# Linear blocks on one core: v's projection in two pieces around the attention's product, and chunk 1's high products ahead of the low ones

## The chip, the cores and the metric

The kernel runs on one core of a Trainium2 chip. The metric is the device time of one execution in microseconds (us). Before the change three timed runs took 3326.6, 3329.98 and 3334.91 us, so the median is 3329.98 us.

## The reference

The program computes four layers on 16 sequences of 512 tokens of width 128. The change touches only the third, a stack of eight blocks of linear attention with a feed-forward part:

```python
for i in range(8):                       # NUM_BLOCKS; D = 128, FF = 512
    residual = x
    Q = fmap(x @ Wq[i] + bq[i])          # fmap(t) = elu(t) + 1
    K = fmap(x @ Wk[i] + bk[i])
    value = x @ Wv[i] + bv[i]
    KV = einsum('nsh,nsh->nh', K, value)
    Ksum = sum(K, axis=1)
    Z = 1.0 / (Q * Ksum[:, None, :] + 1e-6)
    V = Q * KV[:, None, :] * Z
    attn_out = gelu(V @ Wo[i] + bo[i])
    x = _ln(attn_out + residual, ln1_s[i], ln1_b[i])
    residual = x
    h = gelu(x @ W1[i] + b1[i])
    ff_out = gelu(h @ W2[i] + b2[i])
    x = _ln(ff_out + residual, ln2_s[i], ln2_b[i])
```

## The kernel before

`linear_blocks` (from line 2471) holds each sequence of the state as a tile of 128 features x 512 tokens in `XC`. There are 8 blocks x 16 sequences = 128 steps g, and one program for each engine, written as `part(g, old, on)`. They run as a software pipeline of six stages: in step g the engines project q, k and v of item g, do the attention's output and first norm of item g - 1, the second half of that norm and the feed-forward part of item g - 2, its last chunk and y2 of g - 3, the second norm of g - 4, and the last scaling and the write of the state of g - 5. `on(k)` says that item g - k exists. The order of the calls in `part` is the order of the engine's instructions; nothing reorders them. Semaphores order the engines against each other.

On TensorE (PE), a step is, before the change: k's and q's projection (each three fp32r products of 512 columns: high x high, high x low, low x high part; `project`, L2620 to L2622), z1's turn (`turn_z1`, four transposes into M1, L2654), v's projection, the last chunk of the feed-forward output of g - 3 (`down`, L2703), the attention's product wo (`attention_out`, one f32 product, recorded as two, L2662), chunk 0's two high products (`up_high`, L2688, L2689), z2's turn (`turn_z2`, L2675), chunk 0's low product (`up_low`, L2694), the same for chunk 1, y2's turn (L2647) and y1's turn (L2668), chunks 2 and 3, and three chunks of `down`.

What the other engines do in a step, as far as it is spoken of below:
- ScalarE (ACT): lt and rt (a logarithm and an exponential), the exponentials ek and eq (L2788, L2793), a table load (L2796), ao, the gelu of wo's product in M1 (L2802), the write of the state from M2 (XC, L2808), then the gelus of h and ff.
- VectorE (DVE): z1 (L2939), att (L2956), x1 out of z1's turn in M1 (L2964), z2 (L2939), ek's minimum (L2974), eq's minimum (L2976), fk (L2978), eq + 1 (L2981), kv with V (L2984), the statistics of y1 in M1 (L2931, L2934), fq (L2992), the statistics of y2 in M2.
- GpSimd (POOL): the high part of a state (L2860), the high and the low half of x1 (L2870, L2873), y1 = ao + state (L2886), the low part of the state (L2863), the powers for the norms (L2850, L2852), y2 (L2897).

Three tiles in PSUM are used by turns. M1 holds z1's turn, wo's product and y1's turn; `attention_out` waits for `x1_ready` before it writes M1. M2 holds z2's and y2's turn; `turn_y2` waits for `x_ready`, the write of the state. H has two halves, for even and odd chunks. V is waited for by kv on VectorE and, through `v_filled`, by POOL one step later and by SyncE once in a block: it loads the next block's `wqkv` (L3060) when all 16 projections of v are done.

Of the kernel before, what the change touches and what calls it, by code (L numbers as in the profile page):

```python
# [37 lines left out]
def ds(start, size):  # L38
    return bass.ds(start, size)
# [2431 lines left out]
def linear_blocks(nc, C, R, XC, NBLK, NB):  # L2471
# [8 lines left out]
    with ExitStack() as ctx:  # L2480
        def sb(name, shape, dt=F32):
            return ctx.enter_context(nc.sbuf_tensor("lb_" + name, shape, dt))

        def ps(name, shape, dt=F32):
            return ctx.enter_context(nc.psum_tensor("lb_" + name, shape, dt))

        def sem(name):
            return C["sems"].enter_context(nc.semaphore("lb_" + name))

        prm = sb("prm", [P, NPRM, NBLK + 1])  # L2490
        wqkv = sb("wqkv", [P, 2, 3, P], F32R)
# [33 lines left out]
        V = ps("V", [P, 512])  # L2525
# [13 lines left out]
        v_filled = sem("v_filled")  # L2539
# [40 lines left out]
        W, tern_loaded = C["ff_weights"], C["ff_loaded"]  # L2580
        MAGIC = 1.5 * 2.0 ** 23

        def block_of(i):
            return i // NB if isinstance(i, int) else i >> SHIFT
# [5 lines left out]
        def part_of_x(i, low):  # L2590
            par = i % 2 if isinstance(i, int) else i & 1
            return xs[:, ds(par, 1), low, :].rearrange("p a n -> p (a n)")
# [19 lines left out]
        def reused(i):  # L2612

            return not (isinstance(i, int) and i == 0)

        def pe_program(pe):
            def project(W, i, out, signal):


                pe.matmul(out, wqkv[:, 0, W, :], part_of_x(i, 0), start=True, stop=False)  # L2620
                pe.matmul(out, wqkv[:, 0, W, :], part_of_x(i, 1), start=False, stop=False)
                pe.matmul(out, wqkv[:, 1, W, :], part_of_x(i, 0), start=False, stop=True  # L2622
                          ).then_inc(signal, 1)

            def project_k(g):
                pe.wait_ge(wqkv_loaded, 16 * block_of(g) + 16)
                pe.wait_ge(xs_ready, g + 1)
                if reused(g):
                    pe.wait_ge(fk_ready, g)
                project(1, g, K[:, :], k_filled)  # L2630

            def project_q(g):
                if reused(g):
                    pe.wait_ge(fq_ready, g)
                project(0, g, Q[:, :], q_filled)

            def project_v(g):
                if reused(g):
                    pe.wait_ge(kv_ready, g)
                project(2, g, V[:, :], v_filled)  # L2640

            def turn_y2(i):
                pe.wait_ge(y2_ready, i + 1)
                if reused(i):
                    pe.wait_ge(x_ready, i)
                for t in range(NT):
                    last = pe.transpose(M2[:, t * P:(t + 1) * P], y2[:, t * P:(t + 1) * P],  # L2647
                                        C["ident"][:, :])
                last.then_inc(y2_turned, 1)

            def turn_z1(i):
                pe.wait_ge(z1_ready, i + 1)
                for t in range(NT):
                    last = pe.transpose(M1[:, t * P:(t + 1) * P], z1[:, t, :], C["ident"][:, :])  # L2654
                last.then_inc(z1_turned, 1)

            def attention_out(i):
                pe.wait_ge(wo_loaded, 16 * block_of(i) + 16)
                if reused(i):
                    pe.wait_ge(x1_ready, i)  # L2660
                pe.wait_ge(att_ready, i + 1)
                pe.matmul(M1[:, :], wo[:, :], att[:, :], start=True, stop=True  # L2662
                          ).then_inc(o_filled, 1)

            def turn_y1(i):
                pe.wait_ge(y1_ready, i + 1)
                for t in range(NT):
                    last = pe.transpose(M1[:, t * P:(t + 1) * P], y1[:, t * P:(t + 1) * P],  # L2668
                                        C["ident"][:, :])
                last.then_inc(y1_turned, 1)  # L2670

            def turn_z2(i):
                pe.wait_ge(z2_ready, i + 1)
                for t in range(NT):
                    last = pe.transpose(M2[:, t * P:(t + 1) * P], z2[:, t, :], C["ident"][:, :])  # L2675
                last.then_inc(z2_turned, 1)

            def up_high(i, k):
                if k == 0:
                    pe.wait_ge(w1_loaded, 16 * block_of(i) + 16)  # L2680
                    pe.wait_ge(x1_high_ready, i + 1)
                    if reused(i):
                        pe.wait_ge(h_ready, KC * i - 1)
                if k == 1 and reused(i):
                    pe.wait_ge(h_ready, KC * i)
                if k >= 2:
                    pe.wait_ge(h_ready, KC * i + k - 1)
                pe.matmul(H[:, k % 2, :], w1[:, 0, k, :], x1s[:, 0, :], start=True, stop=False)  # L2688
                pe.matmul(H[:, k % 2, :], w1[:, 1, k, :], x1s[:, 0, :], start=False, stop=False)  # L2689

            def up_low(i, k):
                if k == 0:
                    pe.wait_ge(x1_low_ready, i + 1)
                pe.matmul(H[:, k % 2, :], w1[:, 0, k, :], x1s[:, 1, :], start=False, stop=True  # L2694
                          ).then_inc(h_filled, 1)

            def down(i, k):
                if k == 0:
                    pe.wait_ge(w2_loaded, 16 * block_of(i) + 16)
                    if reused(i):  # L2700
                        pe.wait_ge(ff_ready, i)
                pe.wait_ge(h_ready, KC * i + k + 1)
                pe.matmul(FF[:, :], w2[:, k, :], h[:, k, :], start=(k == 0),  # L2703
                          stop=(k == KC - 1)).then_inc(ff_filled, 1)

            def part(g, old, on):
                if on(0):
                    project_k(g)
                    project_q(g)
                if on(2):  # L2710
                    turn_z1(g - 2)
                if on(0):
                    project_v(g)
                if on(3):
                    down(g - 3, KC - 1)
                if on(1):
                    attention_out(g - 1)
                if on(2):
                    up_high(g - 2, 0)
                if on(5):  # L2720
                    turn_z2(g - 5)
                if on(2):
                    up_low(g - 2, 0)
                    up_high(g - 2, 1)
                    up_low(g - 2, 1)
                if on(4):
                    turn_y2(g - 4)
                if on(1):
                    turn_y1(g - 1)
                if on(2):  # L2730
                    for k in range(2, KC):
                        up_high(g - 2, k)
                        up_low(g - 2, k)
                    for k in range(KC - 1):
                        down(g - 2, k)

            def ternary(k):
# [20 lines left out]
                if k == 3:  # L2758
# [4 lines left out]
                    last.then_inc(wfcT_filled, 1)  # L2763

            steps(pe, part, ternary)

        def act_program(act):
# [283 lines left out]
        with nc.Block() as block:  # L3051
            @block.sync
            def _(sp):
# [21 lines left out]
                for k in range(1, NBLK):  # L3075
                    load(k, True)

            block.tensor(pe_program)
            block.scalar(act_program)
            block.gpsimd(pool_program)  # L3080
# [144 lines left out]
```

## Time and profile before

| | us |
|---|---|
| timed runs, median (lowest to highest) | 3329.98 (3326.6 to 3334.91) |
| the profiled execution | 3320.53 |
| its span, first to last instruction | 3318.8 |
| TensorE busy in the span | 2971.5 (90%) |
| VectorE busy | 2598.0 (78%) |
| ScalarE busy | 2294.1 (69%) |
| GpSimd busy | 2071.2 (62%) |
| mean granted TensorE clock | 0.940 |

The page of the profile gives the busy time of each engine, a strip of 40 slices of the span, the chain that ended last and the costliest groups of instructions. The timeline view gives instructions in order of time. Where an instruction waits inside its engine for a way to memory, its record is longer; where it waits for a semaphore, the engine is idle before it and the bracket at the end of the row names what ended that. Times in a row are microseconds from the start of the span.

### The profile page before, as it was taken

Reading aid. Unit: us, or ns where it says so; the run is one execution under the profiler, and the core shown is the slowest. Engines: PE = TensorE matmul, PEld = TensorE weight load, DVE = VectorE, ACT = ScalarE, POOL = GpSimd, SP = SyncE. Lnnn points to the kernel's source line nnn. Section 1 sums busy time; section 2 is a strip of 40 time slices with the busy share of each in tenths; the row PEclk is TensorE's granted clock in tenths of the full one; section 3 lists DMA queues with packets and bytes.
Section 4 is the critical chain, followed back from the end, with each engine's and each line's share of the span. In section 5 each row is a group of like instructions: output and inputs, shape, how many; then the busy total and the mean of one; then the engine's idle time right before and its main releaser. Section 6 shows DMA issues by size and latency. Waiting matters only on the chain. (4 is left out here: it accounts for less than half of the span.)

```text
span 3318.8 us, 65954 instructions
## 1 busy us (share of the span) xinstructions
PE 2971.5 (90%) x22194; PEld 1843.6 (56%) x22194; DVE 2598.0 (78%) x7048; ACT 2294.1 (69%) x3519; POOL 2071.2 (62%) x2319
## 2 busy tenths in 40 slices
PE   5999996799898988499259999999999999999979
PEld 2555553344444444388236666666666666666658
DVE  4666663887887875376569999999999999999967
ACT  4877773365665657254468888888888888888833
POOL 3444443234555453377658888888878888888744
PEclk8999997698999999699669999999999999999979
DMA  4445443222222220486310000000000000000001
GB/s 105 114 102 119 114 101 88 61 57 67 52 58 68 65 67 21 100 284 187 99 45 1 16 1 7 11 6 11 1 16 1 16 1 16 1 16 1 1 14 39
DMA packets 178767, 178.12 MB, mean 54 GB/s; under 512 B 18660, under 2 KB 159167, under 8 KB 178334
## 3 DMA queue, kind: packets, MB, share of 16 engines
q1 hardware_dynamic: 169342, 157.03, 19.0%
q0 software_dynamic: 9088, 16.88, 1.5%
q8 instruction: 178, 2.92, 0.4%
q14 instruction: 159, 1.30, 0.1%
HBM read 99.74 MB, written 75.86 MB: 53 GB/s over the span
## 5 line engine op out<-in xcount | busy, mean ns | idle before, releaser
L2703 PE MATMUL lb_FF<-lb_h,lb_w 128*128 128x512 f32 x1024 | 480.7, 591 | 0.0
L2815 ACT ACTIVATE lb_h<-lb_H,lb_prm 128x512 f32<-128x512 f32 x512 | 337.4, 685 | 45.9 <-PE lb_H L2694 43.6
L2939 DVE TENSOR_SCALAR lb_z<-lb_M,lb_mv,lb_rstd 128x128 f32<-128x128 f32 x1024 | 344.9, 399 | 4.0 <-POOL lb_rstd L2852 3.4
L2852 POOL TENSOR_TENSOR lb_rstd<-lb_rstd,half 128x4 f32<-128x4 f32 x256 | 261.2, 1020 | 36.6 <-issue 0.4
L2703 PEld LDWEIGHTS lb_FF<-lb_h,lb_w 128*128 128x128 f32 x1024 | 193.2, 189 | 145.6 <-issue 92.0
L1538 POOL TENSOR_SCALAR_AFFINE_SELECT da_PT<-da_PT 128x1024 f32<-128x1024 f32 x128 | 145.9, 1145 | 197.7 <-ACT da_PT L1468 197.7
L2688 PE MATMUL lb_H<-lb_x1s,lb_w 128*128 128x512 f32 x512 | 264.3, 516 | 5.4 <-issue 5.4
L2931 DVE BATCH_NORM_STATS2 lb_stats<-lb_M 128x6 f32<-128x128 f32 x1024 | 225.2, 280 | 23.2 <-PE lb_M L2647 14.6
L559 ACT ACTIVATE ga_PT<-ga_S 128x384 f32<-128x384 f32 x256 | 111.7, 489 | 178.5 <-PE ga_S L375 178.5
L1473 ACT ACTIVATE da_PT<-da_SY 128x1536 f32<-128x1536 f32 x128 | 185.2, 1447 | 70.6 <-PE da_SY L1343 69.4
L2886 POOL TENSOR_TENSOR lb_y<-lb_ao,XC 128x512 f32<-128x512 f32 x128 | 192.9, 1507 | 38.3 <-ACT lb_ao L2802 38.1
L2694 PE MATMUL lb_H<-lb_x1s,lb_w 128*128 128x512 f32 x512 | 214.3, 419 | 1.1 <-POOL lb_x1s L2873 1.0
L2008 POOL DMA_INDIRECT moe_ys<-moe_y,moe_dest x156 | 158.1, 1014 | 75.9 <-issue 44.2
L408 PE MATMUL ga_O<-ga_PT,ga_V 128*32 128x512 f32 (+3 forms) x2048 | 202.9, 471 | 0.0
L2689 PE MATMUL lb_H<-lb_x1s,lb_w 128*128 128x512 f32 x512 | 202.6, 396 | 0.0
L1355 PE MATMUL da_O<-da_PT,da_V 128*32 128x128 f32 (+2 forms) x3584 | 191.1, 325 | 3.8 <-ACT da_PT L1473 2.3
L375 PE MATMUL ga_S<-ga_qT,ga_kT 51*128 51x128 bf16 (+2 forms) x1792 | 140.9, 250 | 43.6 <-DVE ga_bm L781 29.8
L2863 POOL TENSOR_TENSOR lb_xs<-XC,lb_xs 128x512 fp32r<-128x512 f32 x128 | 165.7, 1295 | 20.3 <-issue 20.0
L375 PEld LDWEIGHTS ga_S<-ga_qT,ga_kT 51*128 51x128 bf16 x1792 | 69.8, 98 | 194.5 <-issue 110.0
L2873 POOL TENSOR_TENSOR lb_x1s<-lb_x,lb_x1s 128x512 fp32r<-128x512 f32 x128 | 163.5, 1278 | 20.7 <-issue 20.7
L688 POOL DMA_INDIRECT moe_xs<-ga_rows,slot x128 | 128.4, 1003 | 75.7 <-issue 41.6
L784 DVE TENSOR_REDUCE ga_bm<-ga_S 128x8 f32<-128x1024 f32 x128 | 156.1, 1219 | 21.1 <-PE ga_S L399 18.7
(365 smaller groups left out, 8815.9 us busy)
## 6 DMA issues: line engine op xcount, KB each, us to landing
moe_w<-experts_dram SPq DMA_DIRECT2D x39, 384.0 KB, 3.4
da_qT<-da_stq SPq DMA_DIRECT2D x64, 192.0 KB, 4.4
da_kT<-da_stk SPq DMA_DIRECT2D x64, 192.0 KB, 5.5
ga_qT<-ga_stq SPq DMA_DIRECT2D x32, 384.0 KB, 5.9
moe_x<-moe_xs SPq DMA_DIRECT2D x39, 258.0 KB, 4.0
tc_g<-moe_ys SPq DMA_DIRECT2D x32, 256.0 KB, 3.3
lb_split<-moe_parts SPq DMA_DIRECT2D x8, 896.0 KB, 6.0
da_stq<-da_parts SPq DMA_DIRECT2D x16, 384.0 KB, 2.4
```

The source lines that it names most:

```text
L375: last = pe.matmul(bank[:, o:o + cols], k[:, j * P:(j + 1) * P], q[:, q0:q0 + cols], start=(part > 0), stop=(part > 0 or j == 3), skip_gro ...
L408: last = pe.matmul(O[32 * c:32 * c + 32, j * P:SEQ], V[:, (n // 4) % BUF, j, n % 4, :], PT[:, (2 * n + c // 2) % RING, at:at + NT - j, :]. ...
L1355: last = pe.matmul(O[32 * c:32 * c + 32, q0:q0 + cols], V[:, (n // 4) % 2, j, 2 * (n % 4) + c % 2, :], PT[:, (2 * n + c // 2) % RING, c % ...
L2688: pe.matmul(H[:, k % 2, :], w1[:, 0, k, :], x1s[:, 0, :], start=True, stop=False)
L2689: pe.matmul(H[:, k % 2, :], w1[:, 1, k, :], x1s[:, 0, :], start=False, stop=False)
L2694: pe.matmul(H[:, k % 2, :], w1[:, 0, k, :], x1s[:, 1, :], start=False, stop=True).then_inc(h_filled, 1)
L2703: pe.matmul(FF[:, :], w2[:, k, :], h[:, k, :], start=(k == 0), stop=(k == KC - 1)).then_inc(ff_filled, 1)
L2815: act.activation(h[:, k, :], H[:, k % 2, :], ACT.Gelu_apprx_tanh, bias=col(FB1 + k, i)).then_inc(h_ready, 1)
L2852: pool.tensor_tensor(out[:, :], out[:, :], C["half"][:, 0:NT], ALU.pow).then_inc(done, 1)
L2886: pool.tensor_tensor(y1[:, :], ao[:, :], state(i), ALU.add).then_inc(y1_ready, 1)
L2931: v.bn_stats(stats[:, t, :], M[:, t * P:(t + 1) * P])
L2939: last = v.tensor_scalar(z[:, t, :], M[:, t * P:(t + 1) * P], mv[:, t, 0:1], rstd[:, t:t + 1], ALU.subtract, ALU.mult)
```

## The change

Only TensorE's program changes. `project` is split into `project_begin` (the first product) and `project_end` (the other two). In a step:
- the last chunk of `down` for g - 3 comes ahead of v's projection,
- v's first product stays ahead of the attention's product, the other two go behind chunk 0's low product,
- chunk 1's two high products go ahead of chunk 0's low product; between chunk 0's high products and z2's turn nothing changes, so z2's turn is now followed by chunk 1's high products.

```diff
         def pe_program(pe):
-            def project(W, i, out, signal):
-
-
+            def project_begin(W, i, out):
                 pe.matmul(out, wqkv[:, 0, W, :], part_of_x(i, 0), start=True, stop=False)
+
+            def project_end(W, i, out, signal):
                 pe.matmul(out, wqkv[:, 0, W, :], part_of_x(i, 1), start=False, stop=False)
                 pe.matmul(out, wqkv[:, 1, W, :], part_of_x(i, 0), start=False, stop=True
                           ).then_inc(signal, 1)
+
+            def project(W, i, out, signal):
+                project_begin(W, i, out)
+                project_end(W, i, out, signal)
...
-            def project_v(g):
+            def begin_v(g):
                 if reused(g):
                     pe.wait_ge(kv_ready, g)
-                project(2, g, V[:, :], v_filled)
+                project_begin(2, g, V[:, :])
+
+            def end_v(g):
+                project_end(2, g, V[:, :], v_filled)
...
                 if on(2):
                     turn_z1(g - 2)
-                if on(0):
-                    project_v(g)
                 if on(3):
                     down(g - 3, KC - 1)
+                if on(0):
+                    begin_v(g)
                 if on(1):
                     attention_out(g - 1)
                 if on(2):
...
                 if on(5):
                     turn_z2(g - 5)
                 if on(2):
+                    up_high(g - 2, 1)
                     up_low(g - 2, 0)
-                    up_high(g - 2, 1)
+                if on(0):
+                    end_v(g)
+                if on(2):
                     up_low(g - 2, 1)
                 if on(4):
                     turn_y2(g - 4)
```

## Rows read from the trace of the kernel before

**Rows 1.** Busy time of each engine over one linear block, 16 steps.

```profile
core 0: us, PE busy (x) PEld busy (x) DVE busy (x) ACT busy (x) POOL busy (x), PEclk, DMA share, GB/s
2587.58:2767.95 180.37, 179.87 (x753) 117.49 (x753) 170.93 (x545) 155.89 (x209) 144.58 (x160) 1.00 0.03 8
```

**Rows 2.** Timeline of one step; start us, duration us, instruction, count, idle time before.

```profile
2586.26 0.60 PE L2654 MATMUL lb_M<-ident,lb_z 128*128 128x128 f32 x4
...
2586.89 0.81 DVE L2964 TENSOR_SCALAR lb_x<-lb_M,lb_prm 128x512 f32<-128x512 f32 x1
...
2588.25 1.02 PE L2662 MATMUL lb_M<-lb_att,lb_wo 128*128 128x512 f32 x2
...
2588.54 1.27 POOL L2873 TENSOR_TENSOR lb_x1s<-lb_x,lb_x1s 128x512 fp32r<-128x512 f32 x1 [0.16 <-issue]
...
2588.90 1.20 DVE L2974 TENSOR_SCALAR lb_ek<-lb_ek 128x512 f32<-128x512 f32 x1
...
2589.31 0.69 ACT L2802 ACTIVATE lb_ao<-lb_M,lb_prm 128x512 f32<-128x512 f32 x1 [0.85 <-PE lb_M L2662]
...
2590.02 0.41 DVE L2976 TENSOR_SCALAR lb_eq<-lb_eq 128x512 f32<-128x512 f32 x1
...
2590.07 1.50 POOL L2886 TENSOR_TENSOR lb_y<-lb_ao,XC 128x512 f32<-128x512 f32 x1 [0.26 <-ACT lb_ao L2802]
2590.21 0.78 ACT L2808 ACTIVATE XC<-lb_M,lb_prm 128x512 f32<-128x512 f32 x1 [0.21 <-PE lb_M L2675]
...
2590.71 0.39 PE L2694 MATMUL lb_H<-lb_x1s,lb_w 128*128 128x512 f32 x1
...
2591.13 0.63 PE L2647 MATMUL lb_M<-ident,lb_y 128*128 128x128 f32 x4
...
2591.63 0.66 PE L2668 MATMUL lb_M<-ident,lb_y 128*128 128x128 f32 x4
...
2595.70 0.80 PE L2620 MATMUL lb_K<-lb_xs,lb_wqkv 128*128 128x512 f32 x1
```

**Rows 3.** Timeline of the drain, where PE waits for x1 ahead of wo.

```profile
3138.83 0.80 DVE L2964 TENSOR_SCALAR lb_x<-lb_M,lb_prm 128x512 f32<-128x512 f32 x1
...
3139.74 1.10 PE L2662 MATMUL lb_M<-lb_att,lb_wo 128*128 128x512 f32 x2 [0.16 <-issue]
```

**Rows 4.** Timeline of an early step without z2, VectorE and GpSimd.

```profile
1719.83 0.42 DVE L2974 TENSOR_SCALAR lb_ek<-lb_ek 128x512 f32<-128x512 f32 x1
1719.97 0.74 POOL L2870 CAST lb_x1s<-lb_x 128x512 fp32r<-128x512 f32 x1 [2.91 <-DVE lb_x L2964]
1720.16 0.83 DVE L2976 TENSOR_SCALAR lb_eq<-lb_eq 128x512 f32<-128x512 f32 x1
1720.88 1.28 POOL L2873 TENSOR_TENSOR lb_x1s<-lb_x,lb_x1s 128x512 fp32r<-128x512 f32 x1 [0.16 <-issue]
...
1721.75 0.69 DVE L2981 TENSOR_SCALAR lb_eq<-lb_eq 128x512 f32<-128x512 f32 x1
1722.11 1.48 POOL L2886 TENSOR_TENSOR lb_y<-lb_ao,XC 128x512 f32<-128x512 f32 x1
```

**Rows 5.** The lines of eq and y1, 1750 to 3135 us; duration ns min/median/max.

```profile
L2976 DVE TENSOR_SCALAR lb_eq<-lb_eq x123: 412/414/1541, 1755.4 to 3130.9; 128x512 f32<-128x512 f32 x123
...
L2886 POOL TENSOR_TENSOR lb_y<-lb_ao,XC x123: 1287/1517/1524, 1755.4 to 3130.9; 128x512 f32<-128x512 f32 x123
```

**Rows 6.** Timeline of the one step with the long eq.

```profile
2473.36 0.80 DVE L2964 TENSOR_SCALAR lb_x<-lb_M,lb_prm 128x512 f32<-128x512 f32 x1
...
2476.45 1.29 POOL L2886 TENSOR_TENSOR lb_y<-lb_ao,XC 128x512 f32<-128x512 f32 x1 [0.17 <-ACT lb_ao L2802]
2476.48 1.54 DVE L2976 TENSOR_SCALAR lb_eq<-lb_eq 128x512 f32<-128x512 f32 x1
...
2484.79 0.65 PE L2654 MATMUL lb_M<-ident,lb_z 128*128 128x128 f32 x4 [0.84 <-DVE lb_z L2939]
...
2485.48 0.81 DVE L2964 TENSOR_SCALAR lb_x<-lb_M,lb_prm 128x512 f32<-128x512 f32 x1
```

**Rows 7.** The loads of wqkv (L3060), seven of them, time from issue to landing.

```profile
L3060 SPq DMA_DIRECT2D lb_wqkv<-lb_split x7: 530/530/531, 1865.6 to 2948.2; - x7
...
DMA to landing us min/median/max: 3.4/3.5/3.6
```

## The prediction

> **What bounds the kernel now.** I first read the page's table of busy time (TensorE leads, VectorE follows) and its strip of 40 slices, to find where the touched code runs: it is the linear blocks, from about 1700 to 3180 us. Then the busy time of each engine over one linear block of 16 steps [rows 1]: 180.37 us, so 11.27 us a step, TensorE busy for 179.87 of them at a granted clock of 1.00, and VectorE for 170.93. Both are nearly full, and with that the share of busy time has told all it can: what counts is which wait ends last inside one step, and that only the timeline shows.
>
> One step is laid out in [rows 2]. I count from the end of x1 on VectorE, 2586.89 + 0.81 = 2587.70, and call that time 0.
> - TensorE (PE) waits twice. Its own beat is 0.23 us for a 512-wide fp32r product. From the last product of chunk 1 (2590.71) to y2's turn (2591.13) it takes 0.42, so 0.19 is a wait: ScalarE's write of the state (2590.21 + 0.78 = 2590.99) must free M2. Its group of four takes 0.63 against 0.60 of an undisturbed one, 0.03 more. y1's turn starts 0.50 after y2's, where four transposes need 0.44 to 0.45 (0.36 to the next record and 0.08 in the longer first product behind them), and takes 0.66: 0.05 and 0.06 more. In sum 0.33 a step, so PE alone would need 11.27 - 0.33 = 10.94.
> - POOL and VectorE wait for each other. x1's low half is on POOL from 0.84 to 2.11. VectorE's ek (min, SBUF to SBUF) starts at 1.20 and takes 1.20, until 0.29 after that low half ends. The same instruction takes 0.42 where POOL is idle at its start [rows 4]. Then VectorE starts eq at 2.32, done in 0.41, and POOL starts y1 at 2.37 and needs 1.50 for it; where nothing stood in its way it takes 1.29 [rows 5]. So eq has the way into SBUF first and y1 stands behind it, by a margin of 0.05 us.
>
> **The change part by part.** It adds and removes no instruction; the same matmuls and waits are issued in another order, and no DMA is issued by this engine.
> 1. *down's last chunk ahead of v's projection.* They swap, and both are ready: down's h was finished before. Nothing.
> 2. *Two of v's three products behind the attention's product.* wo starts 2 x 0.23 = 0.46 earlier on PE's own beat: 2588.25 - 2586.26 = 1.99 after z1's turn before, 1.53 now. But it overwrites M1, which x1 reads, and x1 ends 1.44 after z1's turn. What such a wait costs is seen in the drain, where PE comes to wo early [rows 3]: x1 ends at 3139.63, wo is recorded at 3139.74 and takes 1.10 instead of 1.02, so it runs 0.19 after x1's end. wo now runs at 0.19 instead of 0.55: 0.10 of new wait, and 0.36 earlier relative to x1. In line behind it: H's products, z2's turn and the rest of PE, and ScalarE's ao.
> 3. *v finished later.* VectorE multiplies with V only after eq, fk and eq + 1, over 1 us after v's new end. SP's load of the next block's wqkv waits for it too. v's last product is now followed by a low product, y2's turn and all that lay between y2's turn and K's next product, 2595.70 - 2591.13 = 4.57 before [rows 2]; with 0.23 in front and 0.16 for the product's own drain, some 4.6 us. The load lands 3.4 to 3.6 us after its issue [rows 7]. Hidden, with about 1 us left, seven times in all. Were it not, it would be a few tenths each time.
> 4. *z2's turn and chunk 1's high products ahead of the low ones.* x1's low half is needed at 2.11 + about 0.2; the product stands at 0.19 + 0.86 + 0.46 + 0.44 + 0.46 = 2.41. No wait. z2's turn ends 0.36 to 0.46 earlier, so the state is written earlier, and the wait of 0.19 ahead of y2's turn goes.
>
> So PE's own sum is a gain: 10.94 + 0.10 = 11.04 against 11.27. What decides is what the earlier wo triggers on the other engines. ao now ends 0.36 earlier, at 0.19 + 1.02 + 0.04 + 0.69 = 1.94, and y1 can be asked for at 1.94 + 0.07 = 2.01. That is before x1's low half ends (2.11), so y1 stands in POOL's queue directly behind it, and 0.31 us *before* VectorE's eq at 2.32, where it came 0.05 behind it.
>
> Who gets the way when an instruction of each waits is shown by an early step [rows 4]. At 1721.75 VectorE's eq + 1 waits behind x1's low half (to 1722.16), with y1 directly behind that on POOL (recorded from 1722.11): VectorE is through at 1722.44, and y1 ends at 1723.59, 1.15 later. So ek passes ahead of y1, as now. And at 1719.97 POOL's cast waits behind ek, VectorE's eq follows at 1720.16: the cast goes first, to 1720.71, and eq ends only at 1720.99, in 0.83. So y1 passes ahead of eq. eq then waits for the end of y1, 2.40 + 1.15 = 3.55, and ends near 3.8 instead of 2.73; fk, eq + 1, kv, the statistics, z1, z1's turn and the next x1 all stand behind it. Behind eq comes one more such wait, of eq + 1 behind the low half of the state.
>
> This price needs no sum of parts, since it happened once in the profiled run. Of 123 eq's in the steady steps the median is 414 ns and one took 1541 [rows 5]. It is the one at 2476.48, with y1 in front of it by 0.03 us [rows 6]; PE then waits 0.84 us for z1, and from that step's x1 (2473.36) to the next (2485.48) pass 12.12 us instead of 11.27. There the next step had PE's late wo again and recovered. After the change wo is bound to x1 (0.19 behind it), and VectorE's sequence from x1 to ek and eq is bound to x1 too, so the order is the same in every step and the delay doesn't heal. Nor does PE's slack help: whatever wait PE gets ahead of z1's turn, x1 and wo shift together.
>
> The sum: 12.12 - 11.27 = 0.85 us x 123 steps = 105 us, less the one that was there already, 104. The few steps before (no z2 between x1 and ek) and the drain have another alignment: nothing, or tenths. The profiled execution took 3320.53 (span 3318.8), so 3424.5. The median of the timed runs is 9.5 above it; if that is of lost turns such as the one at 2476 (11 of them would do), the changed kernel has them anyway and stays at 3424, if it comes from elsewhere, 3434. I take 3430.
>
> The Trainium skill, "SBUF — State Buffer", section "Who interferes with whom", says that VectorE and GpSimd share one pair of SBUF ports as an exclusive lock, that a two-port tensor_scalar takes it, and that whoever issues first holds it for a whole instruction. The trace agrees (ek's 1.20 against 0.42), and by that rule eq's loss follows from y1's earlier issue; it does not say who is next when both wait. By its sentence that PE and ACT never wait on anyone alone, a reader counting PE's waits would arrive at the gain of the first rival below.
>
> **The rivals.**
> - *PE's own sum holds (faster).* eq keeps its place ahead of y1. The step is then 11.04, a saving of 0.23 x 123 = 28 us: 3302. For it: PE is the fullest engine, and eq follows ek on VectorE without a gap, so it might take the way along. Against it: the cast that went ahead of eq in [rows 4], and the 0.31 us. It decides from the point where y1 is asked for after 2.32, that is if ao ends over 0.3 us later than I lay out.
> - *POOL gets both turns (slower still).* y1 passes ahead of ek as well. y1 runs to 3.4, ek to 3.7, then the low half of the state is queued before eq and goes first, to 4.8; eq ends near 5.1. Even without a wait at eq + 1 this is about 0.97 us a step more than my case: 3430 + 119 = 3549. Against it: [rows 4] has VectorE through first behind that very pair.
> - *A mixed pattern.* Turns lost in some steps only, as hiccups shift the phases: anything between 3310 and 3400.
> - *The wqkv load shows.* Even 1 us each time is 7 us, within my range.
>
> **How the numbers follow.** My case 0.82, PE's own sum 0.10, both turns lost 0.05, mixed 0.03. The range of my case: a step of 12.0 to 12.3 (the event of [rows 6] had a delayed ScalarE and could be off by that much either way) is 90 to 127 us on 3320.5 to 3330, or 3410 to 3457; with the scatter of the timed runs (3326.6 to 3334.9) 3405 to 3465. It holds nearly all of the 0.82, so 8 in 10. 0.3% is 10 us, about what a measurement of this kernel can tell from no change. Faster by more: 0.10, the first rival. Within: 0.02 of the mixed case. Slower: 0.88.
>
> **What would show it.** Right: eq (the first tensor_scalar after ek) takes about 1.5 us in nearly all of the 123 steps, y1 starts within 0.05 of the end of x1's low half, z1's turn shows a wait for VectorE of about 0.8 us a step, the wait ahead of y2's turn is gone, a block takes 194 us, and PE's busy share of it falls to about 93%. Wrong: eq stays at 0.41, and a block takes 176.6. If ek takes 2.4, POOL has both turns. A wait of K's first weight load for wqkv once a block would show step 3 wrong.

## The result, and the profile after

| us | before | after |
|---|---|---|
| timed runs beside each other, median (lowest to highest), six of each | 3330.35 (3326.6 to 3334.91) | 3442.03 (3436.19 to 3444.01) |
| the profiled execution | 3320.53 | 3444.01 |
| its span | 3318.8 | 3442.3 |
| from x1 to x1, median of the steady steps | 11.27 | 12.12 |
| from the fifth x1 to the 126th | 1364.3 | 1469.8 |

The ratio of the times is 1.0332, with a 95% interval of 1.0319 to 1.0346: the changed kernel is slower by 112 us.

The page after, its table of busy time: engine, busy us (share of the span), instructions.

```profile
span 3442.3 us, 65954 instructions
PE 2988.9 (87%) x22194; PEld 1842.6 (54%) x22194; DVE 2725.7 (79%) x7048; ACT 2312.0 (67%) x3519; POOL 2048.6 (60%) x2319
```

TensorE computes what it did before (2989 us against 2972) in a longer span. VectorE has the same 7048 instructions, and 128 us more of busy time: the first sign that its instructions became longer, not more. One block of 16 steps between two loads of wqkv, like [rows 1] (that was the fifth such block, this is the first; the six of them take 193.9 to 194.9 us after and 180.2 to 181.2 before):

```profile
core 0: us, PE busy (x) PEld busy (x) DVE busy (x) ACT busy (x) POOL busy (x), PEclk, DMA share, GB/s
1890.48:2084.36 193.88, 180.08 (x753) 116.67 (x752) 187.42 (x545) 158.25 (x209) 141.59 (x161) 1.00 0.03 7
```

A block went from 180.37 to 193.88 us, at the same granted clock of 1.00. PE's busy time is what it was (180.08 against 179.87), so PE now stands idle for 13.8 us of a block; VectorE is busy for 16.5 us more. POOL is busy for 3 us less. Two groups of the lines view name the instruction (duration in ns, least/median/most, first and last start, shapes); they answer to [rows 5]:

```profile
L2986 DVE TENSOR_SCALAR lb_eq<-lb_eq x124: 422/1518/1522, 1755.2 to 3250.3; 128x512 f32<-128x512 f32 x124
L2896 POOL TENSOR_TENSOR lb_y<-lb_ao,XC x125: 1287/1477/1490, 1757.2 to 3261.9; 128x512 f32<-128x512 f32 x125
```

eq's minimum had a median of 414 ns and one case of 1541; now 1518 is the median. One step of the timeline after, to be laid beside [rows 2] (start us, duration us, instruction, idle time before and what ended it):

```profile
2347.59 0.66 PE L2661 MATMUL lb_M<-ident,lb_z 128*128 128x128 f32 x4 [0.85 <-DVE lb_z L2949]
...
2348.29 0.81 DVE L2974 TENSOR_SCALAR lb_x<-lb_M,lb_prm 128x512 f32<-128x512 f32 x1
...
2349.20 1.10 PE L2669 MATMUL lb_M<-lb_att,lb_wo 128*128 128x512 f32 x2
...
2349.94 1.28 POOL L2883 TENSOR_TENSOR lb_x1s<-lb_x,lb_x1s 128x512 fp32r<-128x512 f32 x1 [0.16 <-issue]
...
2350.29 1.22 DVE L2984 TENSOR_SCALAR lb_ek<-lb_ek 128x512 f32<-128x512 f32 x1
2350.34 0.69 ACT L2812 ACTIVATE lb_ao<-lb_M,lb_prm 128x512 f32<-128x512 f32 x1 [1.30 <-PE lb_M L2669]
...
2351.18 1.48 POOL L2896 TENSOR_TENSOR lb_y<-lb_ao,XC 128x512 f32<-128x512 f32 x1
2351.24 0.78 ACT L2818 ACTIVATE XC<-lb_M,lb_prm 128x512 f32<-128x512 f32 x1 [0.22 <-PE lb_M L2682]
...
2351.43 1.52 DVE L2986 TENSOR_SCALAR lb_eq<-lb_eq 128x512 f32<-128x512 f32 x1
...
2352.45 0.60 PE L2654 MATMUL lb_M<-ident,lb_y 128*128 128x128 f32 x4
...
2352.82 1.29 POOL L2873 TENSOR_TENSOR lb_xs<-XC,lb_xs 128x512 fp32r<-128x512 f32 x1 [0.16 <-issue]
...
2353.70 0.70 DVE L2991 TENSOR_SCALAR lb_eq<-lb_eq 128x512 f32<-128x512 f32 x1
...
2354.98 0.88 DVE L2941 BATCH_NORM_STATS2 lb_stats<-lb_M 128x6 f32<-128x128 f32 x4
...
2359.72 0.66 PE L2661 MATMUL lb_M<-ident,lb_z 128*128 128x128 f32 x4 [0.85 <-DVE lb_z L2949]
2360.41 0.81 DVE L2974 TENSOR_SCALAR lb_x<-lb_M,lb_prm 128x512 f32<-128x512 f32 x1
```

Count again from x1's end, 2348.29 + 0.81 = 2349.10. wo ends at 1.20, ao at 1.93, and y1 starts at 2.08, while x1's low half is still ending on POOL (2.12). VectorE comes to eq at 2.33, which is 0.25 *behind* y1, where before it was 0.05 ahead. y1 ends at 3.56, eq at 3.85, 0.29 later. Before, eq ended at 2.73. Everything behind eq on VectorE shifts, and the brackets of z1's turn show where it comes out: PE waits 0.85 us for VectorE's z1, and so it does in nearly every step. From x1 to the next x1 pass 12.12 us.

eq ends 1.12 later than before, and yet the step is only 0.85 longer: VectorE had time to spare. Two more rows of the step of [rows 2], the statistics of y1 and the next x1:

```profile
2592.45 0.88 DVE L2931 BATCH_NORM_STATS2 lb_stats<-lb_M 128x6 f32<-128x128 f32 x4
...
2598.14 0.81 DVE L2964 TENSOR_SCALAR lb_x<-lb_M,lb_prm 128x512 f32<-128x512 f32 x1
```

Before, the statistics start 4.75 behind x1's end and the next x1 ends 6.50 behind their start; after, it is 5.88 and 6.24 (in the median of the steps 4.76 and 6.51, and 5.88 and 6.24). With a short eq VectorE's own round would thus take 4.76 + 6.24 = 11.00 us, an estimate from these rows. That is 0.27 less than the 11.27 in which PE's order set the pace; after the change the 0.27 are used up, and 1.12 - 0.27 = 0.85.

### The profile page after: what moved, and what is told of

Same layout as the page of the kernel before. It is cut to its first block and busy times, and to the rows that moved or that the text cites. A ratio compares the mean times of both kernels' runs of the same rounds, so it can differ in the third digit from the quotient of the medians.

```text
span 3442.3 us, 65954 instructions
## 1 busy us (share of the span) xinstructions
PE 2988.9 (87%) x22194; PEld 1842.6 (54%) x22194; DVE 2725.7 (79%) x7048; ACT 2312.0 (67%) x3519; POOL 2048.6 (60%) x2319
## 5 line engine op out<-in xcount | busy, mean ns | idle before, releaser
L2825 ACT ACTIVATE lb_h<-lb_H,lb_prm 128x512 f32<-128x512 f32 x512 | 352.8, 689 | 46.0 <-PE lb_H L2701 43.0
L2695 PE MATMUL lb_H<-lb_x1s,lb_w 128*128 128x512 f32 x512 | 257.8, 504 | 5.4 <-issue 5.4
L2710 PEld LDWEIGHTS lb_FF<-lb_h,lb_w 128*128 128x128 f32 x1024 | 183.9, 190 | 134.2 <-issue 91.9
L2860 POOL TENSOR_TENSOR lb_rstd<-lb_mv,lb_eps 128x4 f32<-128x4 f32 x256 | 52.6, 206 | 294.1 <-DVE lb_mv L2944 294.1
L2696 PE MATMUL lb_H<-lb_x1s,lb_w 128*128 128x512 f32 x512 | 203.7, 398 | 0.0
L2701 PE MATMUL lb_H<-lb_x1s,lb_w 128*128 128x512 f32 x512 | 201.9, 395 | 0.8 <-POOL lb_x1s L2883 0.8
L2812 ACT ACTIVATE lb_ao<-lb_M,lb_prm 128x512 f32<-128x512 f32 x128 | 88.1, 689 | 165.2 <-PE lb_M L2669 165.2
L2986 DVE TENSOR_SCALAR lb_eq<-lb_eq 128x512 f32<-128x512 f32 x128 | 189.0, 1476 | 0.9 <-ACT lb_eq L2803 0.8
L2661 PE MATMUL lb_M<-ident,lb_z 128*128 128x128 f32 x512 | 84.2, 287 | 111.6 <-DVE lb_z L2949 111.6
```

What stands on the lines that cost most here:

```text
L2825: act.activation(h[:, k, :], H[:, k % 2, :], ACT.Gelu_apprx_tanh, bias=col(FB1 + k, i)).then_inc(h_ready, 1)
L2986: v.tensor_scalar(eq[:, :], eq[:, :], 1.0, -1.0, ALU.min, ALU.add)
```

## The experiments

Two theories were to be told apart. *The lock:* VectorE's eq loses its place at a shared way into SBUF to GpSimd's y1, because wo comes earlier, and nothing else in the change costs anything. *The rivals:* the other half of the change (the high products ahead of the low one) costs time, v's later end does, or VectorE is simply full. Kernels that ran beside each other are compared through the kernel before in the same set. In the first set (e1, e2, e3, e5) that took 3382.5 us: the stages ahead of the linear blocks were some 50 us longer there for every kernel, so the time from x1 to x1 is the cleaner measure. y1's start is counted from x1's end, like all times within a step.

| kernel | ratio to before (95%) | x1 to x1, us | eq, median ns | y1's start, us |
|---|---|---|---|---|
| before | 1 | 11.27 | 414 | 2.37 |
| after | 1.0332 (1.0319 to 1.0346) | 12.12 | 1518 | 2.08 |
| e1_v_split_only | 1.0313 (1.0273 to 1.0354) | 12.11 | 1516 | 2.08 |
| e2_high_first_only | 0.9997 (0.9974 to 1.0021) | 11.26 | 414 | 2.37 |
| e3_y1_behind_ek | 0.9994 (0.9974 to 1.0014) | 11.27 | 414 | 2.53 |
| e5_eq_beside_psum | 1.0010 (0.9987 to 1.0033) | 11.27 | 677 | 2.08 |
| e4_gate_and_chunk2 | 0.9979 (0.9966 to 0.9993) | 11.14 | 414 | 2.54 |
| e6_two_v_gate_chunk2 | 0.9979 (0.9968 to 0.9990) | 11.17 | 414 | 2.54 |
| e7_two_v_no_gate | 1.0328 (1.0310 to 1.0347) | 12.12 | 1514 | 2.15 |
| e8_one_product | 0.9938 (0.9925 to 0.9952) | 11.05 | 414 | 2.54 |
| e9_one_product_no_gate | a single run: 3438.5 beside 3329.0 | 12.12 | 1517 | 2.08 |

### Which half of the change costs the time

e1 is the changed kernel with chunk 1's high products back behind chunk 0's low one; v stays in two pieces.

```diff
                 if on(2):
-                    up_high(g - 2, 1)
                     up_low(g - 2, 0)
+                    up_high(g - 2, 1)
                 if on(0):
                     end_v(g)
```

> Part of the change alone: v's projection in two pieces and down's last chunk first, but chunk 0's low product again ahead of chunk 1's high ones. My theory (the earlier wo puts y1 ahead of eq at the shared way into SBUF): wo is as early as in the changed kernel, so y1 is too; a step takes 12.12 us, eq about 1.5 us, the time is that of the changed kernel, 3442 within 6. Rival (the new order of H's products makes the loss): 3330. Rival (only both together do): 3330.

e2 is the other half alone: the kernel before, with chunk 1's high products ahead of chunk 0's low one, and v in one piece.

```diff
                 if on(2):
+                    up_high(g - 2, 1)
                     up_low(g - 2, 0)
-                    up_high(g - 2, 1)
```

> The other part alone: v's projection whole and in its old place, chunk 1's high products ahead of chunk 0's low one. My theory: wo, ao and y1 stay where they were, eq keeps its 0.41 us and a step its 11.27 us, since z2's turn starts no earlier and y2's turn still waits for the state: 3330 within 5. Rival (the order of H's products makes the loss): 3442. If z2's turn ahead of more work were worth the 0.19 us of y2's wait: 3307.

The group of eq in the lines view, first of e1, then of e2:

```profile
L2986 DVE TENSOR_SCALAR lb_eq<-lb_eq x123: 419/1516/1523, 1807.5 to 3290.3; 128x512 f32<-128x512 f32 x123
```

```profile
L2976 DVE TENSOR_SCALAR lb_eq<-lb_eq x128: 411/414/1526, 1759.8 to 3186.6; 128x512 f32<-128x512 f32 x128
```

The whole loss comes with the split of v's projection, which is what brings wo forward, and none of it with the order of the products: 12.11 and 1516 ns in one, 11.26 and 414 ns in the other. e2 is no faster than the kernel before, either: the product order alone gives nothing at 11.26.

### Taking the early turn from y1

e3 is the changed kernel, with one wait more: GpSimd doesn't start y1 before VectorE's ek of the step has ended. PE's order is that of the change.

```diff
+        ek_done = sem("ek_done")
...
+                    if on(0):
+                        pool.wait_ge(ek_done, g + 1)
...
-                    v.tensor_scalar(ek[:, :], ek[:, :], 1.0, None, ALU.min)
+                    v.tensor_scalar(ek[:, :], ek[:, :], 1.0, None, ALU.min).then_inc(ek_done, 1)
```

> TensorE's order of the changed kernel, untouched; POOL's y1 also waits for VectorE's ek, so it can't be asked for before about 2.45 us after x1's end, behind eq's start at 2.32. My theory: eq is back at 0.41 us, y1 ends 3.88 after x1's end, y1's turn stands at 3.78 in TensorE's order and waits 0.2, so a step takes 11.04 + 0.2 = 11.25 us and the time is 3328 within 8. Rival (the late v or wo's wait for x1 makes the loss, the long eq only stands in that slack): a step stays at 12.12, 3442.

Timeline of one step of e3:

```profile
2353.18 0.81 DVE L2977 TENSOR_SCALAR lb_x<-lb_M,lb_prm 128x512 f32<-128x512 f32 x1
...
2354.09 1.10 PE L2670 MATMUL lb_M<-lb_att,lb_wo 128*128 128x512 f32 x2
...
2356.31 0.41 DVE L2989 TENSOR_SCALAR lb_eq<-lb_eq 128x512 f32<-128x512 f32 x1
...
2356.52 1.35 POOL L2899 TENSOR_TENSOR lb_y<-lb_ao,XC 128x512 f32<-128x512 f32 x1 [0.41 <-issue]
...
2357.32 0.60 PE L2655 MATMUL lb_M<-ident,lb_y 128*128 128x128 f32 x4
...
2357.93 0.65 PE L2676 MATMUL lb_M<-ident,lb_y 128*128 128x128 f32 x4
...
2364.43 0.81 DVE L2977 TENSOR_SCALAR lb_x<-lb_M,lb_prm 128x512 f32<-128x512 f32 x1
```

wo starts as early as in the changed kernel (0.10 after x1's end in the record, 1.10 long), and ao is as early. Only y1 is held, until 2.53 (the profile puts that wait down to "issue"), and eq has its 0.41 back; the step is 11.25 from x1 to x1 here, 11.27 in the median. y1 starts 0.45 later than after the change, and yet the kernel is 0.85 us a step faster: an instruction that starts *later* on one engine pays for the other. So y1's early turn is the cause, and not an early wo, a late v or a full VectorE as such.

### Taking eq off the shared way

e5 leaves y1 as early as it is, and changes what eq reads. In the changed kernel both eq steps read and write SBUF only; here each has a second operand in PSUM, which is what fk has. The kernel leaves out the step of 1 down and up again and bounds eq by the larger of Q and 1, so it computes another eq and is of use for its time alone.

```diff
-                    v.tensor_scalar(eq[:, :], eq[:, :], 1.0, -1.0, ALU.min, ALU.add)
+                    v.scalar_tensor_tensor(out=eq[:, :], in0=Q[:, :], scalar=1.0,
+                                           in1=eq[:, :], op0=ALU.max, op1=ALU.min)
...
-                    v.tensor_scalar(eq[:, :], eq[:, :], 1.0, None, ALU.add)
+                    v.scalar_tensor_tensor(out=eq[:, :], in0=Q[:, :], scalar=0.0,
+                                           in1=eq[:, :], op0=ALU.mult, op1=ALU.add)
```

> TensorE's and POOL's order of the changed kernel, untouched. VectorE's two steps on eq are two-operand instructions of which one operand lies in PSUM (as fk's and kv's do), in place of the SBUF-to-SBUF ones; they leave out the subtraction and addition of 1 and bound eq in another way. My theory: such an instruction doesn't stand behind POOL, so eq takes 0.75 us instead of 1.52 and eq + 1 0.75 with no wait; from x1 to kv 0.4 us more than in the kernel before, a step of 11.4 us, 3346 within 10, though y1 is as early as in the changed kernel. Rival (y1's early start hurts in another way, or v's or wo's place does): 12.12 us, 3442. If every VectorE instruction with an SBUF operand stands behind POOL: 12.2 or more.

Timeline of one step of e5:

```profile
2344.42 0.81 DVE L2974 TENSOR_SCALAR lb_x<-lb_M,lb_prm 128x512 f32<-128x512 f32 x1
...
2346.07 1.28 POOL L2883 TENSOR_TENSOR lb_x1s<-lb_x,lb_x1s 128x512 fp32r<-128x512 f32 x1 [0.16 <-issue]
...
2346.42 1.21 DVE L2984 TENSOR_SCALAR lb_ek<-lb_ek 128x512 f32<-128x512 f32 x1
...
2347.31 1.48 POOL L2896 TENSOR_TENSOR lb_y<-lb_ao,XC 128x512 f32<-128x512 f32 x1
...
2347.55 0.68 DVE L2986 SCALAR_TENSOR_TENSOR lb_eq<-lb_Q,lb_eq 128x512 f32<-128x512 f32 x1
...
2355.68 0.81 DVE L2974 TENSOR_SCALAR lb_x<-lb_M,lb_prm 128x512 f32<-128x512 f32 x1
```

y1 is where the changed kernel has it, running from 2347.31 to 2348.79. eq starts 0.24 us into it and is done in 0.68 us, in the middle of y1's run. ek, still an instruction from SBUF to SBUF, has its 1.21 as ever. So what eq waits for is not GpSimd being busy but a way that the form from SBUF to SBUF needs and the one with an operand in PSUM doesn't, and 12.12 falls to 11.27 though y1 stays early.

The Trainium skill, "SBUF — State Buffer", section "Who interferes with whom", says of the pair of ports that VectorE shares with GpSimd that it is an exclusive lock, and that a VectorE instruction outside the two-port modes with at most one input in SBUF doesn't contend for it. The trace agrees: eq took 0.68 us beside y1 with one input in PSUM, and 1.52 with its input in SBUF alone.

The expectation had 11.4, and it came to 11.27. It had counted 0.4 us more up to kv, and that came to 0.27: eq's own 0.26 in full, and next to nothing for eq + 1, which takes 0.69 here and took 0.68 in the kernel before too, where it stood behind y1. The statistics of y1 then start 5.02 behind x1's end, and 5.02 + 6.24 = 11.26. So VectorE sets the pace of e5, and that its step is as long as the one before the change, where PE set it, is a coincidence.

### What PE's order is worth once y1 is held

With e3, PE's early start gave nothing: 11.27, as before. In its rows y1 ends at 2356.52 + 1.35 = 2357.87, and PE's turn of y1 starts at 2357.93, 0.61 behind y2's turn, where [rows 2] has 0.50 and undisturbed transposes 0.44: PE's next wait is for y1 itself. e4 covers that with work: chunk 2's two high products go between y2's turn and y1's turn.

```diff
                 if on(4):
                     turn_y2(g - 4)
+                if on(2):
+                    up_high(g - 2, 2)
                 if on(1):
                     turn_y1(g - 1)
                 if on(2):
-                    for k in range(2, KC):
-                        up_high(g - 2, k)
-                        up_low(g - 2, k)
+                    up_low(g - 2, 2)
+                    up_high(g - 2, 3)
+                    up_low(g - 2, 3)
```

> The kernel of e3 (the changed order, y1 held until ek is done) with chunk 2's two high products ahead of y1's turn, to fill TensorE's wait for y1 of 0.2 us a step. My theory: eq stays at 0.41 us; what is left on TensorE is its own 10.94 and wo's wait for x1 of 0.10, so a step of 11.04 us, 0.23 less than before in each of 123, some 28 us: ratio 0.9915 to before. If VectorE's own round is longer than I count (it was at 11.27 in two kernels, before and e3, which TensorE's waits explain as well), it stays at 11.27, ratio 1.00.

It came to 11.14 a step, and the time is lower than before by 0.21% (0.07 to 0.34). The missing 0.1 is in these rows of one step of e4:

```profile
2655.73 0.74 DVE L2999 SCALAR_TENSOR_TENSOR lb_kv<-lb_V,lb_prm,lb_fk 128x512 f32<-128x512 f32 x1
...
2655.87 0.60 PE L2676 MATMUL lb_M<-ident,lb_y 128*128 128x128 f32 x4
2656.40 0.08 DVE L2999 DVE_READ_ACCUMULATOR lb_kv<-lb_V,lb_prm,lb_fk 128x1 f32 x1
2656.50 0.89 DVE L2946 BATCH_NORM_STATS2 lb_stats<-lb_M 128x6 f32<-128x128 f32 x4
```

VectorE's statistics of y1 start 0.10 behind the read of kv's accumulator (0.12 in the median of the steps), where before they start with it, and they stand right behind the end of y1's turn (2655.87 + 0.60). In PE's order y1's turn now comes two products, 0.46 us, later (4.25 behind x1's end, against 3.94 in e3), and that is more than VectorE had to spare: 4.88 + 6.24 = 11.12, all but the 11.14.

e6 looks for the rest elsewhere, in the 0.10 of wait at wo: e4, with two of v's three products ahead of wo.

```diff
             def project_begin(W, i, out):
                 pe.matmul(out, wqkv[:, 0, W, :], part_of_x(i, 0), start=True, stop=False)
+                pe.matmul(out, wqkv[:, 0, W, :], part_of_x(i, 1), start=False, stop=False)
...
             def project_end(W, i, out, signal):
-                pe.matmul(out, wqkv[:, 0, W, :], part_of_x(i, 1), start=False, stop=False)
```

> e4 with two of v's three products ahead of wo and one behind chunk 0's low product. wo stands at 0.32 us after x1's end and waits for nothing, but chunk 2's high products now come 0.1 us earlier than h's first chunk is done. My theory: a step of 11.0 to 11.1 us, ratio 0.9905 to 0.994. If wo's wait for x1 of 0.10 us is all that matters: 10.98, ratio 0.990.

It gave nothing, 11.17: y1's turn starts at 4.29 and the statistics at 4.93, and 4.93 + 6.24 = 11.17. e7 is the same edit on the changed kernel, without the wait for ek and without chunk 2's move. It brings wo forward by only one product, and so asks where the threshold is.

> The changed kernel with two of v's three products ahead of wo, nothing held. It asks where it decides: wo then runs 0.32 us after x1's end (0.19 in the changed kernel, 0.55 before), so y1 is asked for at 2.14, still ahead of eq's 2.32. My theory: lost turn in every step, 12.12 us, ratio 1.032 to before. Rival (the loss grows with how much of v is late): about a half of it, 1.016.

```profile
L2986 DVE TENSOR_SCALAR lb_eq<-lb_eq x122: 419/1514/1524, 1752.0 to 3221.3; 128x512 f32<-128x512 f32 x122
```

y1 starts at 2.15, against 2.37 before, and the loss is the whole one, 12.12. There is no middle: of the 123 steady steps the turn is lost in 122 (here, in the changed kernel, in e1 and in e9 alike) or, with y1 at 2.37 and later, in one or none. The step with the long eq in [rows 6] narrows it down: y1 started there at 2476.45 - 2474.16 = 2.29, and eq lost. So the point lies between 2.29 and 2.37, with eq's own start, 2.32, between them.

The one steady step that kept the turn in the changed kernel gained little by it. GpSimd came 0.4 us late to x1's low half there, so ek and eq found the way free, 0.42 us each; but PE then waited 0.41 for that low half, VectorE waited 0.77 for v, and the step still took 11.98 us. In that step alone VectorE waited for v.

e8 moves half as much as e4: only the first of chunk 2's two high products goes ahead of y1's turn, the second comes behind it. The edit is shown against the changed kernel; y1's wait for ek is that of e3.

```diff
+                if k != 2:
+                    up_high_rest(k)
+
+            def up_high_rest(k):
                 pe.matmul(H[:, k % 2, :], w1[:, 1, k, :], x1s[:, 0, :], start=False, stop=False)
...
+                if on(2):
+                    up_high(g - 2, 2)
                 if on(1):
                     turn_y1(g - 1)
                 if on(2):
-                    for k in range(2, KC):
-                        up_high(g - 2, k)
-                        up_low(g - 2, k)
+                    up_high_rest(2)
+                    up_low(g - 2, 2)
+                    up_high(g - 2, 3)
+                    up_low(g - 2, 3)
```

> e4 with only the first of chunk 2's high products ahead of y1's turn. In e4 a step took 11.136 us, not 11.04, and VectorE's statistics of y1 started 0.12 us late, behind y1's turn that two products had pushed back. My theory: y1 is ready 3.99 us after x1's end, TensorE comes to its turn at 4.01, the statistics wait no more, and a step takes 11.02 to 11.06 us: 0.1 less than e4, ratio 0.991 to 0.994 to before (e4 measured 0.998). Rival (e4's 11.136 is VectorE's own round, the 0.12 only moves elsewhere): 11.13, ratio 0.998.

Timeline of one step of e8:

```profile
2299.21 0.81 DVE L2984 TENSOR_SCALAR lb_x<-lb_M,lb_prm 128x512 f32<-128x512 f32 x1
...
2302.34 0.41 DVE L2996 TENSOR_SCALAR lb_eq<-lb_eq 128x512 f32<-128x512 f32 x1
2302.55 1.35 POOL L2906 TENSOR_TENSOR lb_y<-lb_ao,XC 128x512 f32<-128x512 f32 x1 [0.42 <-issue]
...
2304.03 0.60 PE L2676 MATMUL lb_M<-ident,lb_y 128*128 128x128 f32 x4
...
2304.78 0.08 DVE L3004 DVE_READ_ACCUMULATOR lb_kv<-lb_V,lb_prm,lb_fk 128x1 f32 x1
2304.78 0.88 DVE L2951 BATCH_NORM_STATS2 lb_stats<-lb_M 128x6 f32<-128x128 f32 x4
...
2310.25 0.81 DVE L2984 TENSOR_SCALAR lb_x<-lb_M,lb_prm 128x512 f32<-128x512 f32 x1
```

The statistics start with the read of the accumulator again, y1's turn ends 0.15 before them, and x1 comes again after 11.04 us (11.05 in the median), where PE's own sum was 11.04 and VectorE's round 11.00. The medians are 3309.63 and 3328.95 us, the ratio on record 0.9938 (0.9925 to 0.9952): the one version that clearly beats both kernels, by 0.6% the kernel before and, through that one (1.0332 / 0.9938), by some 4% the changed one.

e9 is e8 with GpSimd's wait for ek taken away again, and nothing else.

> e8 without the wait of y1 for ek; nothing else differs. My theory: eq loses its turn in every step, 12.12 us a step, though TensorE's order is the best one found: 1.08 us x 123 = some 130 us above e8. Rival (TensorE's new order of y1's turn also takes the conflict away): as e8.

```profile
2402.89 0.81 DVE L2982 TENSOR_SCALAR lb_x<-lb_M,lb_prm 128x512 f32<-128x512 f32 x1
...
2405.78 1.48 POOL L2904 TENSOR_TENSOR lb_y<-lb_ao,XC 128x512 f32<-128x512 f32 x1
2406.02 1.52 DVE L2994 TENSOR_SCALAR lb_eq<-lb_eq 128x512 f32<-128x512 f32 x1
```

y1 is back at 2.08, eq at 1.52, the step at 12.12 and the time at 3438.5 us. The same PE order is worth 19 us less or 110 us more than the kernel before, by one wait on another engine.

## Why the prediction was right, and where it was off

It forecast 3430 us in 3405 to 3465, and slower at 0.88; the median is 3442.03. The mechanism is the one it named. By its steps:

- *Step 1, down ahead of v: nothing.* Right as far as it can be told: e3 has that swap and ends at 11.27. Alone it wasn't tried.
- *Step 2, wo at 0.19 behind x1's end, and ao at 1.94.* Right. wo is recorded 0.10 after x1's end with 1.10 for its duration, where 1.02 is undisturbed, so it runs at 0.18; ao ends at 1.93.
- *Step 3, v and the wqkv load hidden.* Right. The load issues seven times and lands in 3.4 to 3.7 us (3.4 to 3.6 in [rows 7]), and no instruction of the steady steps waited for it.

```profile
L3070 SPq DMA_DIRECT2D lb_wqkv<-lb_split x7: 529/530/530, 1890.5 to 3057.2; - x7
DMA to landing us min/median/max: 3.4/3.5/3.7
```

- *Step 4, y2's wait goes.* Right: y2's turn is a group of 0.60 without a wait in front, the write of the state having ended 0.43 before it. One low product in all waited for x1's low half, 0.41 us, in the step in which GpSimd was late.
- *y1 asked for at 2.01, and recorded from within 0.05 of the low half's end.* Right: 2.08 against 2.12. *It passes ahead of eq, but not ahead of ek.* Right in 122 of the 123 steady steps: ek has its 1.22. *eq ends near 3.8:* 3.85. *y1 ends at 3.55:* 3.56. *z1's turn waits 0.8:* 0.85. *12.12 a step:* 12.12. *A block of 194, PE at 93%:* 193.88, 92.9%. So the one event of [rows 6] gave the price of the others to a hundredth (the parts that it is made of, the 1.12 of eq less the 0.27 that VectorE had to spare, the prediction didn't take apart), and the order of turns read from [rows 4] held.
- *The first rival, PE's own sum of 11.04.* It is no fiction: it is the state in which e8 runs, at 11.05. e3 shows that the sum alone wasn't enough for it: with eq in its place PE next waits for y1, and without work to cover that the gain of 0.23 is gone. The prediction had left that out. As written (eq keeps its place, so 11.04 and 3302) this rival would have come to 3330, no gain.

Where it was off, by 12 us, is in small terms:
- *The fill, "nothing, or tenths".* From the first K to the fifth x1 it took 2.5 us more (66.0 against 63.5; the other kernels lie between 63.6 and 65.9). The turn is lost once among those steps already, in the last of them, which makes some 0.9 of it; where the rest comes from isn't shown. The drain had 1.1 more.
- *The steady steps, 104.* From the fifth x1 to the 126th it was 105.5. The 0.853 times 121 is 103.2. Most of the rest is a dozen steps of 12.3 to 12.5 us, 3.5 us over the median in all. In each of them one instruction of VectorE (fq, or one of the norms) has idle time of 0.13 to 0.45 us in front, and the row names no releaser. The kernel before has the same gap ahead of the same instruction in the same steps. Of fq, after and before:

```profile
2587.21 0.75 DVE L3002 SCALAR_TENSOR_TENSOR lb_fq<-lb_Q,lb_prm,lb_eq 128x512 f32<-128x512 f32 x1 [0.45 <-issue]
```

```profile
2515.33 0.75 DVE L2992 SCALAR_TENSOR_TENSOR lb_fq<-lb_Q,lb_prm,lb_eq 128x512 f32<-128x512 f32 x1 [0.45 <-issue]
```

Before, those steps took 11.25 to 11.35 us, for VectorE had 0.27 to spare; after, it had nothing, and the gaps show. The prediction left that out: it priced the lost turn and not the slack that goes with it.
- *The median's offset.* Of the two readings of the 9.5 us between profiled execution and median, lost turns or something else, the prediction went between them, at 3430 and not at 3434. The profiles speak for something else: that of before has one lost turn, and so has e2's, in the same step, while the time up to the first K varies from 1696 to 1764 us over all kernels. The profiled execution after had 11.3 of its 123.5 us from there, and 3.0 from the last layer (136.5 us from the last write of the state to the end, against 133.5; the other kernels lie between 133.5 and 136.6). The change touches neither. Medians against medians, 3330.35 + 105.5 + 2.5 + 1.1 = 3439.5, and 2.5 us stay unexplained, within the scatter of the runs.

Of the experiments' expectations three missed. e5 was sized too high, as told there. e4's 11.04 took y1's turn for free: it is, up to one product, and not for two. e6's 11.0 to 11.1 took the wait of 0.10 at wo for something that bounded the step; it was VectorE, behind y1's turn, that did. (The absolute times that were expected of the first set are off by its 50 us, e1's 3442 against 3491.47; the steps and ratios of e1, e2 and e3 came as expected.)

Two things stay open. What the gaps of VectorE in a dozen steps are isn't shown by any row, only that the change didn't make them. And e8's gain was timed in five runs on one chip only; its mechanism rests on the rows above, and not on an experiment that takes it apart further than e9 does.

## What to carry to other kernels

Before moving work earlier on the engine that seems to bound the kernel, follow what it releases through to every engine that shares something, and look how far apart the contenders stand there: here eq's lead of 0.05 us decided 104. Look, too, at what the engine that comes second has to spare (0.27 us a step here): that much comes off the price of a lost turn, and a reordering on the first engine can bring no more than that. A rare long instance of an instruction, one 1541 among 123 of 414, is worth finding in the timeline: it is the price of a state that an edit may make permanent. Where an early producer takes a turn from the critical engine, hold it back by a wait; only then does the reordering pay, and only up to what the next engine has to spare (one product here, not two).

## What the runs showed of the hardware

- The turn at the shared way goes to the one that came first: with VectorE's eq due at 2.32, it was lost with y1 at 2.08 and 2.15 in 122 of 123 steady steps and with y1 at 2.29 in the one step of [rows 6], and kept with y1 at 2.37 and 2.53. The loss doesn't grow by degrees. Nor do the two engines simply alternate: in [rows 2] y1 stood ready at 2.37, before ek ended at 2.40, and eq still went ahead of it.
- An instruction of VectorE that stands behind GpSimd's ends 0.29 us after it, in all three meetings seen here, each of the same form and shape (ek behind the low half, eq behind y1, eq + 1 behind the state's low half: 2354.40 against 2354.11). GpSimd's stands longer: y1 behind eq ends 1.15 after it (2357.87 against 2356.72 in e3), nearly its whole undisturbed 1.29. So the same meeting costs VectorE up to 1.1 us when it loses, and GpSimd 0.06 to 0.21 (1.35 and 1.50 against 1.29) when VectorE's takes 0.41.
- What VectorE's form from SBUF to SBUF saves undisturbed (0.41 against 0.68) is less than what it risks (1.52). A slower form with a PSUM operand took the lost turn out with y1 left at 2.08: 11.27 a step. With y1 elsewhere it wasn't tried.
